# One low part in eight moves from VectorE to GpSimd in the second phase of a two-layer graph kernel

## The reference

```python
gate = ...                                     # from x, per row
view2 = (adj * gate[:, None] * gate[None, :]) @ x_norm       # layer 0
x = layernorm(x + layernorm(fused(x_norm, view2) + x))
support_t = adj @ xt                           # layer 1, xt is a map of x
h = proj(expmap0(support_t)); xt = relu(logmap0(h)); h = proj(expmap0(xt))
x = layernorm(x + h)
```

## Time and profile before

| | us |
|---|---|
| Median of 3 runs | 966.04 (965.82 to 969.86) |
| Profiled execution, its own time | 968.86 |
| Its span, first to last instruction | 967.1 |
| PE busy | 912.5 (94%) |
| DVE busy | 799.9 (83%) |
| ACT busy | 691.1 (71%) |
| POOL busy | 230.7 (24%) |
| Queue of the tile loads, share of 16 DMA engines | 74.3% |

### The profile page before, as it was taken

How to read it: one execution, slowest core, us unless ns; L and a number is a source line. 1 busy time by engine, 2 the same in 40 slices (tenths; PEclk the granted TensorE clock), 3 DMA queues, 4 the chain that set the end, 5 groups by cost and what they waited for, 6 DMA issues and landing times.

```text
span 967.1 us, 12611 instructions
## 1 busy us (share of the span) xinstructions
PE 912.5 (94%) x4052; PEld 724.1 (75%) x4052; DVE 799.9 (83%) x1791; ACT 691.1 (71%) x1224; POOL 230.7 (24%) x202
## 2 busy tenths in 40 slices
PE   5998998999999999999999999998999999899993
PEld 3555777777787877888888888886787778777882
DVE  4667888988898788978695775859999999989995
ACT  5775686868686657757565565655878989788993
POOL 2210211111111111111020010201100755484464
PEclk9999999999999999999999999999999999999997
DMA  6988697786868587868574574756899999899990
GB/s 242 376 289 309 237 401 274 293 309 256 324 242 339 226 306 255 312 219 303 208 277 164 218 288 175 255 196 223 315 376 370 383 388 413 342 376 381 397 361 33
DMA packets 51825, 281.72 MB, mean 291 GB/s; under 512 B 6528, under 2 KB 8496, under 8 KB 20656
## 3 DMA queue, kind: packets, MB, share of 16 engines
q1 hardware_dynamic: 46432, 271.48, 74.3%
q10 hardware_dynamic: 5328, 9.44, 2.6%
HBM read 271.44 MB, written 9.46 MB: 290 GB/s over the span
## 4 chain that ended last, share of the span: by engine, by line
PE 47%; DVE 29%; ACT 8%; DMA 6%; POOL 5%; issue 4%; SPq 0%; POOLq 0%; DVEq 0%; ACTq 0%
PE PS L1007 13%; PE PS L1009 13%; PE PS L1008 13%; DVE AL L742 8%; DVE XGL L742 7%; DMA A<-in_adjT_dram 4%; DVE XTL L742 2%; PE PS L1096 2%; PE PS L1092 2%; DVE BS L691 2%; PE PS L1005 2%; ACT AH L546 1%; POOL r_rs L436 1%; DMA FU<-in_x_dram 1%; POOL p_inv L436 1%
## 5 line engine op out<-in xcount | busy, mean ns | idle before, releaser
L546 ACT ACTIVATE AH<-A 128x1024 fp32r<-128x1024 f32 x251 | 257.3, 1058 | 112.0 <-PE PS L1009 84.6
L742 DVE TENSOR_TENSOR AL<-A,AH 128x1024 fp32r<-128x1024 f32 x251 | 299.4, 1220 | 41.9 <-ACT AH L546 40.8
L742 DVE TENSOR_TENSOR XGL<-A,XGH 128x1024 fp32r<-128x1024 f32 x119 | 139.2, 1217 | 5.0 <-ACT XGH L546 4.9
L1007 PE MATMUL PS<-AH,XGH 128*128 128x512 f32 x344 | 137.5, 400 | 6.2 <-DVE AL L742 6.2
L1009 PE MATMUL PS<-AH,XGL 128*128 128x512 f32 x344 | 134.5, 391 | 0.0
L1008 PE MATMUL PS<-AL,XGH 128*128 128x512 f32 x344 | 134.3, 390 | 0.0
L546 ACT ACTIVATE XGH<-A 128x1024 fp32r<-128x1024 f32 x119 | 118.5, 1056 | 7.9 <-DMA A<-in_adjT_dram 7.8
L1007 PE MATMUL PS<-AH,XTH 128*128 128x512 f32 x298 | 117.9, 396 | 5.5 <-DVE AL L742 5.4
L1009 PE MATMUL PS<-AH,XTL 128*128 128x512 f32 x298 | 116.7, 392 | 0.0
L1008 PE MATMUL PS<-AL,XTH 128*128 128x512 f32 x298 | 116.6, 391 | 0.0
L742 DVE TENSOR_TENSOR XTL<-A,XTH 128x1024 fp32r<-128x1024 f32 x92 | 109.7, 1220 | 4.9 <-ACT XTH L546 4.5
(11 more groups left out here) (242 smaller groups left out, 1545.5 us busy)
## 6 DMA issues: line engine op xcount, KB each, us to landing
A<-in_adjT_dram SPq DMA_DIRECT2D x243, 1024.0 KB, 6.8
GB<-gate_scratch SPq DMA_DIRECT2D x12, 256.0 KB, 3.8
XNT<-xnt_scratch SPq DMA_DIRECT2D x12, 256.0 KB, 4.2
XR<-in_x_dram SPq DMA_DIRECT2D x12, 256.0 KB, 4.9
x_scratch<-X SPq DMA_DIRECT2D x12, 256.0 KB, 7.6
xnt_scratch<-XNT ACTq DMA_DIRECT2D x6, 256.0 KB, 6.2
xnt_scratch<-X1T ACTq DMA_DIRECT2D x6, 256.0 KB, 5.5
XR<-in_x_dram ACTq DMA_DIRECT2D x4, 256.0 KB, 7.3
```

The source lines that it names most:

```text
L546: a.activation(high(m), A[:, n % RING, h * HW:(h + 1) * HW], ACT.Copy).then_inc(S["hi"], 1)
L742: v.tensor_tensor(low(m), A[:, n % RING, h * HW:(h + 1) * HW], high(m).bitcast(F32), ALU.subtract).then_inc(S["lo"], 1)
L1007: p.matmul(acc, hi[:, st], high(m)[:, mv], start=start, stop=False)
```

## The change

POOL makes the low part of every eighth half of the second phase: m = 295, 303, ..., 479, which is 24 halves of 198. All are the second half of their tile. DVE leaves them out. Their completion is counted on a new semaphore `lo_pool`, so `lo` counts only what DVE makes, and every wait for a low part goes through a helper that picks the semaphore by half.

```diff
+POOL_LOW_EVERY = 8
+    POOL_LOW = [m for m in HALVES if m >= 2 * N2 and m % POOL_LOW_EVERY == POOL_LOW_EVERY - 1]
+    POOL_COUNT = {m: i + 1 for i, m in enumerate(POOL_LOW)}
+    LOW_COUNT = {m: sum(1 for k in HALVES if k <= m and k not in POOL_COUNT) for m in HALVES}
...
+        def low_made(eng, m):
+            if m in POOL_COUNT:
+                eng.wait_ge(S["lo_pool"], POOL_COUNT[m])
+            else:
+                eng.wait_ge(S["lo"], LOW_COUNT[m])
...
 (SP, load of tile n)
-                        sp.wait_ge(S["lo"], SPLIT_COUNT[2 * (n - RING) + 1])
+                        low_made(sp, 2 * (n - RING))
+                        low_made(sp, 2 * (n - RING) + 1)
...
 (POOL)
+            def split_low(m):
+                n, h = m // 2, m % 2
+                pool.wait_ge(S["hi"], SPLIT_COUNT[m])
+                pool.nop(nofuse=True)
+                g.tensor_tensor(low(m), A[:, n % RING, h * HW:(h + 1) * HW], high(m).bitcast(F32),
+                                ALU.subtract).then_inc(S["lo_pool"], 1)
             for m in range(last_place(events, results)):
+                if m in POOL_COUNT:
+                    split_low(m)
                 for event, c in events.get(m, []):
...
 (DVE, split_low)
-                if n in WHOLE:
+                if n in WHOLE or m in POOL_COUNT:
                     return
...
 (PE, half m)
-                    pe.wait_ge(S["lo"], SPLIT_COUNT[m])
+                    low_made(pe, m)
```

More of the change, by code:

```diff
@@ L209, in build @@
         for name in (
-                "ld0", "ld1", "ld2", "ld3", "ld4", "ld5", "hi", "lo", "used",
+                "ld0", "ld1", "ld2", "ld3", "ld4", "ld5", "hi", "lo", "lo_pool", "used",
                 "xin0", "xin1", "xin2", "urow", "norm_vecs", "weights", "vecs", "const", "ident_ready",
```

## The result

The changed kernel takes 1000.8 us in the median of 4 runs (995.7 to 1001.3) against 967.6 before (4 runs, one more than in the table above). The ratio is 1.0319 (95% interval 1.0287 to 1.0351), about 31 us. I had forecast 985, some 19 us, with 976 to 995 for the forecast itself and 967 to 1006 for the whole with its rivals. The result lies outside the first range and inside the second.

The account below looks back on a forecast made before the run. DVE was taken to pace the opening, PE the rest with DVE close behind. Lateness 18.5 - 5 old waits + 3.5 opening + 2 clock = +19 us, 985 against the median; forecast's range 976 to 995, 8 in 10 range 967 to 1006.

Parts of the forecast that it names:

- the order: Second phase: POOL works in order, so parts behind its late chains make PE wait; 18.5 us, the main term.
- the hold: POOL's read shuts DVE out 1.9 us per operation, net 0.77; 3.5 us charged in the opening, nothing for 18 later ones.
- starved: Rival: POOL reads in pieces or loses several turns to DVE, ready to done 6.25 us; +39, 1005 us, chance 0.12.
- the signs that I had named: Changed profile: POOL rows of 1.9 us or more, DVE stretched, PE waiting 15 to 20 us for POOL, less for DVE.
- my six halves: Halves 303, 351, 391, 399, 455 and 471, late by 2.0, 5.3, 5.1, 1.5, 1.8 and 2.8 us: 18.5 us.
- The clock: Behind PE's 5 us pauses at halves 351 and 391 the granted clock falls; 1.6 us each, 3.2 possible, 2 taken.
- The relief: DVE loses 24 subtractions at 1.135 us, 27 us: 6.8 in the opening, 20 later; by itself worth at most 16 us.
- the first rival: POOL's long read doesn't hold DVE; the opening gains 5.7 us; +10, 976 us, chance 0.25.
- Operation length: POOL's 128x1024 subtraction, reckoned from its 128x128 and 128x1 rows: 1.9 us, bounds 1.2 and 3.2.
- Relief wins: Rival: gains of 16.3 us in the opening and PE's waits outweigh lateness of 10.6; -6, 960 us, chance 0.18.
- ready to done: Time from POOL's part being ready to its completion: 0.6 us wait plus 1.9, 2.5 us; bounds 1.2 and 6.25.

Follow-up runs that it names:

- the square: Four kernels against the one before: POOL's read at the changed kernel's halves 1.0319, at other halves 1.0171; memsets without a read there 1.0018 and 0.9868.
- wait_memset: Against the kernel before: DVE makes all 198 low parts, POOL does two memsets at the 24 places, PE and SP wait for both; 982.51 us, ratio 1.0156.
- placed_noread: As placed, but POOL's subtraction is replaced by two memsets that read nothing and the 24 low parts are left out; 959.54 us, ratio 0.9868.
- placed: As the changed kernel, but POOL's 24 low parts are of halves with at least 4 us between POOL's previous operation and PE's start; 987.55 us, ratio 1.0171.
- relief: Against the kernel before: the 24 low parts are left out altogether, and PE and SP wait for the high part there; 958.93 us, ratio 0.9918.
- read_nowait: Against the kernel before: DVE makes all low parts; POOL subtracts two 128x1024 operands of its own at the 24 places, nobody waits; 1008.81 us, ratio 1.0425.
- read_256: As read_nowait, but POOL subtracts two operands of 128x256 in place of 128x1024; 977.77 us, ratio 1.0073.
- read_one: As read_nowait, but POOL's operation is a copy of 128x1024 float32, with one operand to read; 979.25 us, ratio 1.0087.

## Why the forecast was right, and which term was mis-sized

The direction, the order and the hold were foreseen, and so was the time in the wide range. But the measured +31 us (997 us by the ratio, 1000.8 by the median) is more than the forecast's own 976 to 995 allowed. It lies in the range of 8 in 10 only because the rival *starved* had stretched that to 1006, and starving didn't make the time here. That is luck. Of the signs that I had named, one failed: PE's waits for DVE should have become shorter, and they grew from 9.5 to 14.1 us.

**The order: right in sum, by two errors that cancel.** I had 18.5 us of lateness, less 5 taken up by old waits, plus 2 for the clock: 15.5. The order measured 1.5% in both rows of the square and 1.56% alone, 14 to 15 us. In wait_memset, the order alone, its terms were 15.1 us of waits for POOL, less 5.0 (PE's waits for DVE fell from 9.5 to 4.5), plus about 5 for the clock (an estimate: half of the 10.4 us that PE worked in two stretches granted 0.50, from 759.3 and from 824.2 us). Of my six halves five were late in the changed kernel as I had said, by 13.6 us together where I had 17.0. Half 399 was not: its part was done 2.4 us before PE got there, PE being late by then. Half 431, which I had counted as safe, was late instead, since POOL's chains in front of it had themselves been pushed by earlier parts (half 423's ended at 881.62, and the next chain began at 881.70).

**The clock: right in kind, too small.** Behind the pauses at 351, 391 and 431 the granted clock was lower. The first line below is the worst place, with PE's idle time before half 391 in it. The others begin where PE went on:

```profile
833.50:840.30 6.80, 4.50 (x11) 3.54 (x12) 5.26 (x3) 3.24 (x5) 6.19 (x5) 0.50 0.53 178
...
768.40:775.00 6.60, 6.60 (x24) 5.35 (x25) 3.84 (x4) 1.52 (x3) 3.00 (x4) 0.74 0.86 319
...
835.80:840.30 4.50, 4.50 (x11) 3.53 (x12) 3.30 (x3) 0.94 (x1) 3.94 (x4) 0.50 0.80 269
...
897.90:902.00 4.10, 4.05 (x11) 3.20 (x12) 4.01 (x7) 4.05 (x7) 3.11 (x3) 0.58 0.78 256
```

A granted 0.50 is the level of 1.2 GHz, after PE had stood idle for 4.4 us. Reckoned as in the prediction, the three cost 0.26 x 6.6 + 0.50 x 4.5 + 0.42 x 4.1 = 5.7 us, and not 2. Before, the clock was 1.00 in all of 735 to 951 us. My price of 1.6 us for a pause was right; I took 2 us in all, where three pauses paid it.

**The relief: too small.** Left alone it is worth 8 us, and in placed_noread 13, at other halves. In the forecast it is netted against the hold: in the 3.5 us of the opening, where the first rival has it as 5.7, and behind the opening in the 14 us that I then left out.

**The hold: right in kind and in its price, and charged in the opening alone. This is the step that failed.** The forecast had 1.9 us per operation, 0.77 net of the relief, and then charged 3.5 us net in the opening and nothing for the 18 operations behind it ("14 us stand against 17 us of DVE idle"). The term of 3.5 us measured 1.7%, 16 to 17 us: that is placed, the kernel with hold and relief and no lateness. It is also the 3.0% of the read less the 1.3% of placed_noread.

The price itself was near. An operation of POOL lasts 2.35 us at least, not 1.9, and stretches a subtraction of DVE by up to 2.23. But not all of them hit one in full. The busy times in the profiles of the changed kernel, of relief and of placed show the mean:

```profile
PE 921.1 (92%) x4052; PEld 726.1 (73%) x4052; DVE 817.8 (82%) x1767; ACT 692.4 (69%) x1224; POOL 295.1 (30%) x226
...
PE 908.4 (95%) x4052; PEld 723.6 (76%) x4052; DVE 774.2 (81%) x1767; ACT 691.6 (72%) x1224; POOL 222.8 (23%) x202
...
PE 914.4 (93%) x4052; PEld 722.9 (73%) x4052; DVE 820.6 (83%) x1767; ACT 692.3 (70%) x1224; POOL 297.2 (30%) x226
```

The first two run the same DVE instructions, 817.8 against 774.2 us: 43.6 us of hold, 1.8 us for each of the 24, most of it on subtractions. Leaving 24 subtractions out had saved 799.9 - 774.2 = 25.7 us. So DVE lost 17.9 us net, where my 24 x 0.77 would be 18.4.

What failed is the cover. I had set 14 of these 18 us against DVE's idle time in the sum of the stretch, and nearly all of it came through. DVE's busy time in placed is 20.7 us above the kernel before, and the time rose by 16 to 17. In read_nowait it was 49.6 us and 41 us of time, in read_256 9.8 and 7, in read_one 16.5 and 8, where half was covered. Why idle time gave so little cover is argued, not shown by a run of its own. In the trace of before, a half's low part was done between 0.05 and 4.2 us ahead of PE, for a third of the halves less than 1 us (I paired DVE's subtractions with PE's halves in their order). A hold of 2.2 us takes such a lead at once, and the idle time that comes later doesn't bring it back.

**Operation length.** I took 1.9 us from a 128x128 row. Half of the figure in the Trainium skill (GPSIMD Engine Reference, section 3.1) is an estimate of 2.25, and the trace has 2.35: the Trainium skill was nearer than my row.

**What POOL holds.** The rule of the Trainium skill (SBUF — State Buffer, "Who interferes with whom") that a DVE instruction with two SBUF inputs and a POOL instruction that reads SBUF shut each other out agrees with every run here. How long they do is another matter. The Trainium skill has "for the whole instruction" in its sentence on DVE's two-port modes, and gives the case of two inputs no length; my prediction had carried it over. Here it doesn't fit. In the kernel before, POOL's inverse root of 128x8 at 762.49 us lasted 1.66 us, and DVE's subtraction that started beside it at 762.92 took its usual 1.23. With 11 such roots (1.66 us and more), no subtraction of DVE lasted over 1.23 us. The holds of read_256, read_one and read_nowait, 0.55, 0.84 and 2.23 us, go with what POOL reads.

**The first rival** (no hold) would have been 976 us; the same without a read came out at 971. **Starved** was wrong for this kernel, whose longest operation was 3.94 us against the 6.25 of that rival, yet the mechanism exists (below). **Relief wins** needed 2.1 us or less from ready to done; here it was 2.35 at least.

**The sum.** By the ratios: order 1.5%, hold 3.0%, and relief -1.3%, together 3.2%. The last is the fourth corner of the square, so this sum closes by construction; what is shown is that the order costs the same with and without the read. Put as the prediction had it: 15.5 for the order against 14 to 15, and 3.5 for hold less relief against 16 to 17.

## What to carry to other kernels

An idle engine isn't free help when its reads shut the partner out: ask how long its operation reads, and charge that time to the partner in full, before counting what the partner is relieved of. Here POOL's read took 1.8 us of DVE's time in the mean to save it 1.1, and the one other placement that I tried didn't mend that. Where a result that others wait for goes into the order of a second engine, look at what stands in front of it there, for the chains that it lengthens as well; moving it to halves where that engine was free gave back 1.5%. And don't count the idle time of a near-full engine as cover by its sum over a stretch: here 17 us of it in the kernel before hid little of what DVE lost (in placed, 20.7 us lost and 16 to 17 us of time).

## What the runs showed of the hardware that I had not expected

POOL can be kept out for long. In read_nowait, one of its operations was issued at 736.30 us and lasted 15.33 us, where its shortest took 2.35. POOL's row, and DVE's timeline beside it:

```profile
736.30 15.33 POOL L499 TENSOR_TENSOR FULL<-XTH,XTL 128x1024 f32<-128x1024 f32 x1 [9.84 <-ACT XGH L571]
```

```profile
737.94 2.35 DVE L767 TENSOR_TENSOR XGL<-A,XGH 128x1024 fp32r<-128x1024 f32 x2
740.21 4.62 DVE L767 TENSOR_TENSOR AL<-A,AH 128x1024 fp32r<-128x1024 f32 x4
744.76 4.62 DVE L767 TENSOR_TENSOR XGL<-A,XGH 128x1024 fp32r<-128x1024 f32 x4
749.30 0.68 DVE L949 COPY GB<-PS 128x512 f32<-128x512 f32 x1
749.90 2.82 DVE L767 TENSOR_TENSOR XGL<-A,XGH 128x1024 fp32r<-128x1024 f32 x1
```

DVE ran ten subtractions without a gap. POOL got in when DVE copied from PSUM at 749.30 (751.63 - 2.35 = 749.28), and the next subtraction then took 2.82 us. So DVE's subtractions can keep POOL out for as long as they follow each other. They don't always: in the changed kernel at 709.75 us POOL got in at the first end of a subtraction, with another right behind it. What decides between the two stays open. It comes back at the same place: POOL's operation there took 13.66 us in read_256 and 13.99 in read_one.

A narrow operation of DVE can be shut out as well. In the same kernel, while POOL's operation of 694.36 us ran until 700.62, DVE took 2.38 us for four columns of one operand, where the same instruction took 0.17 us in the changed kernel at 651.38:

```profile
698.27 2.38 DVE L851 TENSOR_SCALAR r_m2m<-r_m 128x4 f32<-128x4 f32 x1
```

And a write alone costs DVE nothing: beside 48 memsets of 128x1024, its subtractions kept 1.209 to 1.227 us.
